# A twelve-part post-norm decoder on one core: cross attention with two bursts and two shared banks, residual normalisations after all four batch elements, the recurrence's buffers inside the sum buffer

## The reference, cut to what matters

```python
sim = einsum(q, k) * 64 ** -0.5        # 512 queries, 154 keys (155 with the null key)
out = einsum(softmax(sim + mask), v)   # then out @ Wo
```

## Time and profile before

| | us |
|---|---|
| median of 3 runs | 6972.68 (6953.23 to 6976.98) |
| the profiled execution | 6962.96 |
| its span in the profile | 6961.2 |
| PE busy in it | 5716.5 |
| mean granted TensorE clock | 0.867 of full |

### The profile page before, as it was taken

The page is one execution under the profiler, slowest core; times in us unless marked ns, Lnnn a source line. Parts: engine busy times, 40 slices in busy tenths (PEclk is TensorE's granted clock), DMA queues, the critical chain, the costliest instruction groups (busy, mean ns, idle before and its releaser), DMA issues. The chain is left out here.

```text
span 6961.2 us, 111729 instructions
## 1 busy us (share of the span) xinstructions
PE 5716.5 (82%) x40346; PEld 3557.6 (51%) x40346; DVE 3487.7 (50%) x7093; ACT 3180.1 (46%) x9357; POOL 2210.9 (32%) x2229
## 2 busy tenths in 40 slices
PE   3898888998988788787887878877778984788888
PEld 2554455555656465464654646547776552223443
DVE  5341354454555364563645636427884445454433
ACT  3342344444456475574755747534441432244422
POOL 0220000001367274672746727406662220000000
PEclk6899898988999899998999989976666996799987
DMA  1000000000011111111111111100000000000000
GB/s 43 1 1 8 13 1 1 1 1 14 1 35 36 31 40 36 35 36 30 41 36 30 41 30 37 40 16 1 1 1 4 1 6 0 7 1 21 1 0 6
DMA packets 28398, 119.49 MB, mean 17 GB/s; under 512 B 5412, under 2 KB 5928, under 8 KB 26024
## 3 DMA queue, kind: packets, MB, share of 16 engines
q1 hardware_dynamic: 27816, 111.97, 5.8%
HBM read 38.55 MB, written 1.05 MB: 6 GB/s over the span
## 5 line engine op out<-in xcount | busy, mean ns | idle before, releaser
L159 POOL MEMSET norm_eps<- 128x1 f32 x44 | 4.3, 98 | 2237.0 <-POOLq L115 2237.0
L1989 POOL TENSOR_TENSOR local_rot<-local_raw,local_cos 128x512 f32<-128x512 f32 x384 | 487.6, 1270 | 301.2 <-DVE local_raw L2033 301.2
L1992 POOL TENSOR_TENSOR local_other<-local_raw,local_sin 128x256 f32<-128x256 f32 x768 | 557.3, 726 | 60.2
L1931 ACT ACTIVATE ps<-ps,local_negmax 128x96 f32<-128x96 f32 x1536 | 488.3, 322 | 37.3 <-DVE local_negmax L2012 36.4
L1854 PE MATMUL ps<-arena,local_xs 128*128 128x512 f32 x768 | 447.0, 666 | 70.2 <-ACT local_xs L1911 51.4
L1995 POOL TENSOR_TENSOR local_rot<-local_rot,local_other 128x512 f32<-128x512 f32 x384 | 487.2, 1269 | 30.1
L1926 ACT ACTIVATE local_squares<-ps 128x512 f32<-128x512 f32 x384 | 230.7, 601 | 508.9 <-PE ps L1854 508.5
L2019 DVE TENSOR_REDUCE local_norm<-local_squares 128x8 f32<-128x512 f32 x384 | 263.4, 686 | 280.4 <-ACT local_squares L1926 280.4
L544 ACT ACTIVATE attn_probs<-attn_shifted,attn_negmax 128x512 f32<-128x512 f32 x256 | 184.9, 722 | 392.5 <-DVE attn_negmax L587 392.5
L587 DVE CUSTOM_DVE_ANT_0 attn_shifted<-arena,ps 128x512 f32<-128x512 f32 x256 | 176.2, 688 | 331.4 <-PE ps L501 331.4
L1842 PE MATMUL ps<-local_K,local_Q 64*64 64x96 f32 x6144 | 337.0, 249 | 0.0
(11 more groups left out here) (490 smaller groups left out, 13280.3 us busy)
## 6 DMA issues: line engine op xcount, KB each, us to landing
local_V_span<-local_V SPq DMA_DIRECT2D x96, 384.0 KB, 4.0
local_V_span<-local_V SPq DMA_DIRECT2D x96, 256.0 KB, 3.6
arena<-in_L1f_a SPq DMA_DIRECT2D x7, 2176.0 KB, 8.7
local_V_span<-local_V SPq DMA_DIRECT2D x72, 128.0 KB, 2.3
arena<-in_L3f SPq DMA_DIRECT2D x1, 3460.0 KB, 11.1
arena<-in_L1f_f SPq DMA_DIRECT2D x6, 537.5 KB, 4.0
arena<-in_L0f SPq DMA_DIRECT2D x1, 2824.5 KB, 9.8
arena<-in_L0x SPq DMA_DIRECT2D x1, 2049.5 KB, 9.0
```

What stands on the lines that cost most here:

```text
L1931: nc.scalar.activation(scores, scores, ACT.Exp, bias=m.negmax[:, s % 2, u:u + 1], accum_out=m.total[:, s % 2, u:u + 1])\
L1989: link(nc.gpsimd.tensor_tensor(rot, raw, m.cos[:, t, a * DH:(a + 1) * DH].unsqueeze(1) .broadcast_to([P, 8, DH]), ALU.mult))
L1992: link(nc.gpsimd.tensor_tensor(other[:, :, lo:lo + HALF], raw[:, :, HALF - lo:DH - lo], m.sin[:, t, a * DH + lo:a * DH + lo + HALF].unsque ...
```

## The change

The sum of a sublayer is kept for every batch element (`core.sums`, and `core.Y` is the current element's part of it). The 20 calls of `residual_norm` are gone; `residual_norm_all(core, core.sums)` stands once behind `rwkv` and once at the end of each of the four sublayers that `each` runs. In `cross_stage` the bank `TAIL` joins `SHARED`: feed pieces, tail transposes and output projections take two banks by turns, and each waits for the use before the last. The values are issued as one burst of four L936 matmuls and one of four L944 matmuls; the latter now take 64 rows each, with `VT` held twice, multiplied by a 0/1 column (`parity`) that keeps the rows of j = 0 or j = 1. The semaphore waits between the segments are gone. With the mask per batch element (L0x) the mask matmul has one row instead of 128, at partition 0 for i = 0 and 64 for i = 1. ACT takes the exponentials ahead of q. In the state-space mixer `first` and the output `Y` are views of `core.sums`.

```diff
-        self.Y = self.buf("Y", [P, S])
+        self.sums = self.buf("sums", [P, B, S])
...
+        self.Y = self.sums[:, b, :]
...
-def residual_norm(core):
-
-    normalize(core, core.X, core.X, add=core.Y[:, :])
...
-    residual_norm(core)
...
         if feeding(s) is not None:
             uses.append(feeding(s))
+        if 0 <= s - TURN < N:
+            uses.append(("tail", s - TURN, 0))
         if projecting(s) is not None:
             uses.append(("out", projecting(s), 0))
...
-        V, VT = tmp("V", [P, 2, INNER]), tmp("VT", [P, 2, QUAD * DH])
+        V, VT = tmp("V", [P, 2, INNER]), tmp("VT", [P, 2, 2, QUAD * DH])
...
-        freed = dict(read, out=y_done)
+        freed = dict(read, out=y_done, tail=tails_ready)
+        first_half = st.sem("first_half")
...
-        SC, PT, TAIL, OUT, SHARED = core.pairs[0:2], core.ps[4], core.ps[5], core.ps[6], core.ps[7]
+        SC, PT, OUT, SHARED = core.pairs[0:2], core.ps[4], core.ps[5], core.ps[6:8]
+
+        def bank(use):
+            return SHARED[use_at[use] % 2]
...
             def wait_for_bank(use):
-                k = use_at[use] - 1
+                k = use_at[use] - 2
                 if k >= 0:
                     pe.wait_ge(freed[uses[k][0]], count(*uses[k]))
...
-                            row = bias[:, qt if mask == "per_query" else b, :]
+                            part = slice(0, P) if mask == "per_query" else slice(DH * i, DH * i + 1)
+                            row = bias[part, qt if mask == "per_query" else b, :]
                             nc.tensor.matmul(SC[n % 2][:, i, 0:2 * keys].rearrange("p (h k) -> p h k", k=keys),
-                                             unit_bf[:, :], row.unsqueeze(1).broadcast_to([P, 2, keys]), start=True,
-                                             stop=False)
+                                             unit_bf[part, :], row.unsqueeze(1).broadcast_to([row.shape[0], 2, keys]),
+                                             start=True, stop=False)
...
                     if n >= 1:
                         pe.wait_ge(pts_ready, n)
-                        pe.wait_ge(tails_ready, n)
                     for g in range(QUAD):
                         nc.tensor.transpose(PT[:, g * P:(g + 1) * P], probs[:, n % 2, g, :], core.ident)
-                    nc.tensor.transpose(TAIL[:, 0:P], ends[:, n % 2, :, :].rearrange("p g k -> p (g k)"),
+                    wait_for_bank(("tail", n, 0))
+                    nc.tensor.transpose(bank(("tail", n, 0))[:, 0:P], ends[:, n % 2, :, :].rearrange("p g k -> p (g k)"),
                                         core.ident).then_inc(turned, 1)
...
-                    for j in range(2):
-                        cols = slice((2 * (quad % 2) + j) * TILE, (2 * (quad % 2) + j + 1) * TILE)
-                        for i in range(2):
-                            h = QUAD * quad + 2 * j + i
-                            nc.tensor.matmul(OUT[DH * i:DH * i + DH, cols], V[:, b % 2, h * DH:(h + 1) * DH],
-                                             pts[:, n % 2, 2 * i + j, :], start=True, stop=False)
-                        if j == 1:
-                            pe.wait_ge(first_pair, n + 1)
-                        elif n >= 1:
-                            pe.wait_ge(values_done, n)
-                        for i in range(2):
-                            part = slice(32 * (2 * i + j), 32 * (2 * i + j) + tail)
-                            mm = nc.tensor.matmul(OUT[DH * i:DH * i + DH, cols],
-                                                  VT[part, b % 2, quad * DH:(quad + 1) * DH], tails[part, n % 2, :],
-                                                  start=False, stop=True)
-                        mm.then_inc(values_done if j == 1 else first_pair, 1)
+                    def place(i, j):
+                        lo = 2 * (quad % 2) + j
+                        return OUT[DH * i:DH * i + DH, lo * TILE:(lo + 1) * TILE]
+                    pairs = [(i, j) for j in range(2) for i in range(2)]
+                    for i, j in pairs:
+                        h = QUAD * quad + 2 * j + i
+                        nc.tensor.matmul(place(i, j), V[:, b % 2, h * DH:(h + 1) * DH], pts[:, n % 2, 2 * i + j, :],
+                                         start=(j == 0), stop=False)
+                    for i, j in pairs:
+                        part = slice(DH * i, DH * i + DH)
+                        mm = nc.tensor.matmul(place(i, j), VT[part, b % 2, j, quad * DH:(quad + 1) * DH],
+                                              tails[part, n % 2, :], start=False, stop=(j == 1))
+                    mm.then_inc(values_done, 1)
...
         @st.block.scalar
         def _(act):
             for s in STEPS:
-                f = feeding(s)
-                if f is not None and f[0] == "q":
...
                             nc.scalar.activation(powers[:, n % 2, g, :], SC[n % 2][:, i, h * keys:(h + 1) * keys],
                                                  ACT.Exp, bias=negmax[:, n % 2, g:g + 1]).then_inc(exp_ready, 1)
+                f = feeding(s)
+                if f is not None and f[0] == "q":
...
+                    nc.scalar.mul(Q[:, b % 2, i, :], bank(f)[:, :], DH ** -0.5).then_inc(read[kind], 1)
...
-                        mm = nc.vector.tensor_copy(VT[:, b % 2, :], out[:, 0:QUAD * DH])
+                        for j in range(2):
+                            own = core.c("parity")[:, j:j + 1]
...
+                                mm = nc.vector.tensor_scalar(VT[:, b % 2, j, :], out[:, 0:QUAD * DH], own, None, ALU.mult)
...
-        Y = tmp("Y", [P, B, S])
+        Y = core.sums
...
-    first, u = buf("first", [P, 2, 4, B, DN]), buf("u", [P, 2, B, 2, SSM_CHUNK])
+    first = core.sums[:, 0:2, :].rearrange("p k (s b n) -> p k s b n", s=4, b=B)
...
         for b in range(B):
             core.work_on(b)
             f(core, b, arena)
+        residual_norm_all(core, core.sums)
...
             rwkv(core)
+        residual_norm_all(core, core.sums)
```

More of the change, by code:

```diff
@@ L823, in cross_stage @@
         if has_null:
-            null_rows = tmp("null_rows", [P, QUAD * DH])
+            null_rows = tmp("null_rows", [P, 2, QUAD * DH])
             loads += QUAD
@@ L839, in _ @@
                     row = 32 * g + tail - 1
-                    sp.dma_start(null_rows[row:row + 1, :], core.dram["null_v"]).then_inc(loaded, 16)
+                    sp.dma_start(null_rows[row:row + 1, g % 2, :], core.dram["null_v"]).then_inc(loaded, 16)
         @st.block.gpsimd
@@ L845, in _ @@
             if has_null:
-                nc.gpsimd.memset(null_rows[:, :], 0.0).then_inc(zeroed, 1)
+                nc.gpsimd.memset(null_rows[:, :, :], 0.0).then_inc(zeroed, 1)
             pool.wait_ge(zeroed, 1)
@@ L890, in _ @@
                     kind, b, i = f
-                    out = SHARED
+                    out = bank(f)
                     ctx = core.context[:, b, :]
@@ L952, in _ @@
                     for c in range(CHUNKS):
-                        mm = nc.tensor.matmul(SHARED[:, 0:TILE], w("Wo", c * P, (c + 1) * P), oT[:, r % 2, c, :],
+                        mm = nc.tensor.matmul(bank(("out", r, 0))[:, 0:TILE], w("Wo", c * P, (c + 1) * P), oT[:, r % 2, c, :],
                                               start=(c == 0), stop=(c == CHUNKS - 1))
@@ L959, in _ @@
             for s in STEPS:
-                f = feeding(s)
-                if f is not None and f[0] == "q":
-                    kind, b, i = f
-                    act.wait_ge(ready[kind], count(kind, b, i))
-                    if b >= 2:
-                        act.wait_ge(scores_ready, U * (b - 1))
-                    nc.scalar.mul(Q[:, b % 2, i, :], SHARED[:, :], DH ** -0.5).then_inc(read[kind], 1)
                 n = s
@@ L976, in _ @@
                                                  ACT.Exp, bias=negmax[:, n % 2, g:g + 1]).then_inc(exp_ready, 1)
+                f = feeding(s)
+                if f is not None and f[0] == "q":
+                    kind, b, i = f
+                    act.wait_ge(ready[kind], count(kind, b, i))
+                    if b >= 2:
+                        act.wait_ge(scores_ready, U * (b - 1))
+                    nc.scalar.mul(Q[:, b % 2, i, :], bank(f)[:, :], DH ** -0.5).then_inc(read[kind], 1)
                 n = s - TURN
@@ L982, in _ @@
                     nc.scalar.copy(pts[:, n % 2, :, :].rearrange("p g q -> p (g q)"), PT[:, :]).then_inc(pts_ready, 1)
-                    nc.scalar.copy(tails[:, n % 2, :], TAIL[:, 0:P]).then_inc(tails_ready, 1)
+                    nc.scalar.copy(tails[:, n % 2, :], bank(("tail", n, 0))[:, 0:P]).then_inc(tails_ready, 1)
         @st.block.vector
@@ L993, in _ @@
                 dve.wait_ge(loaded, 16 * loads)
-                link(nc.vector.tensor_copy(unit_bf[:, :], core.ident))
+                if mask == "per_query":
+                    link(nc.vector.tensor_copy(unit_bf[:, :], core.ident))
+                else:
```

(22 more changed lines are left out.)

1 line of the change is left out of this document (removed).

## The result

The changed kernel takes 6737.74 us (median of 4 runs, 6726.11 to 6747.94) where the kernel before takes 6973.22 beside it: a ratio of 0.9667, 95% interval 0.9643 to 0.9692, or 235 us less. The forecast was 6787, in a range of 6740 to 6855.

A forecast was written before the change was run, and what follows sets the result against it. PE sets the pace in L0x's steady part; start-ups run at half clock, single normalisations are latency-bound. Terms -34.7 - 6.5 + 3.8 - 57 - 33 - 58 = -185 give 6778 from the profiled 6963.0, forecast 6787 us, range 6740 to 6855.

The forecast's parts named there:

- five pipelined stages for 20: Normalisations: 20 single stages of 128.7 us in all become five pipelined ones summing to 94.0, a gain of 34.7 us.
- L0f's restart: L0f: without a normalisation between them, all elements begin at full clock, 6.5 us gained (nothing to 6.5).
- L3f's restart: L3f: elements may gain as L0f's do without normalisations between them; nothing counted.
- L1a without its normalisations: L1a: ACT must load its square-root table while DVE waits, 3 x 1.3 = 3.8 us lost.
- bursts and mask: Cross attentions: four value bursts become two, 0.28 us per unit, and L0x's one-row mask saves 0.12; 57 us (0 to 66).
- banks and start-ups: Cross attentions: two shared banks remove waits for DVE's copy, 33 us; start-ups without gaps reach full clock, 58 us.
- on the clock: Rival: the clock stays at half in the start-ups, gain 26 instead of 58, 6819 us; chance 0.15.
- on the bank: Rival: the second bank only moves the wait to the tail transpose or q's late read, 6820 us; chance 0.07.
- on the bursts: Rival: the bursts give nothing, 0.15 paid elsewhere or saved time becomes evict and POOL waits, 6844 us; chance 0.10.
- the tail burst's halves run one after the other: Rival: a tail burst takes 1.03 us instead of 0.59, 31 us lost over 192 units, 6875 us; chance 0.03.
- The slower rival: Steady parts: PE waits for DVE and POOL and the clock falls to 1.2 GHz, 7152 us; chance 0.02.
- a sign against the forecast: Cross attentions: the forecast is wrong if, among other signs, L936 and L918 wait more than they do now.

The follow-up runs named there:

- e2: Changed kernel with the value matmuls back in the old order of four segments (two whole rows, two tails, twice): 6804.24 us, ratio 0.9764.
- e4: Changed kernel with L0x's mask again as matmuls over 128 rows, unit matrix as other operand: L0x 294.1 us instead of 287.9, one run.
- e3: Changed kernel with one bank for feed pieces and projections and the other for tail transposes, as before the change: 6836.76 us, ratio 0.9820.
- e1: Changed kernel with the whole cross-attention function as before, so only the normalisations change: 6903.78 us, ratio 0.9917.
- e7: Changed kernel with DVE's eviction ahead of the maxima in cross attentions and L1a's square-root table loaded early: 6716.66 us, ratio 0.9636.
- e10: Kernel of e5 (all value matmuls 128 rows by 64 columns) with the four-segment order of e2: 6728.34 us in one run.
- e8: Changed kernel with one kind of burst per stage all on one part of the array, results wrong, for times only: 6824.6 us in one run.
- e9: Changed kernel with e5's and e7's edits, DVE's total ahead of a feed piece's copy, and split waits for POOL's products: 6708.78 us, ratio 0.9618.
- e6: Changed kernel with each burst reordered, both matmuls of one column half and then both of the other: 6750.59 us in one run.
- e5: Changed kernel with tail value matmuls over 128 rows, using four masked copies of the tail values: 6728.6 us, ratio 0.9654.

## Why the forecast was right, and where it was too small

Term by term, in us, from the profiles; the span fell by 224.4 us:

| term | forecast | measured | from |
|---|---|---|---|
| five pipelined stages for 20 | -34.7 | -40.8 | 128.65 to 87.9, the five windows above |
| L0f's restart | -6.5 | -6.5 | four elements of 43.65 |
| L3f's restart | nothing | -3.0 | its elements, 301.4 to 298.5 |
| L1a without its normalisations | +3.8 | -1.0 | its elements, 811.8 to 810.8 |
| bursts and mask | -57 | -63 | e2 and e4, 56.8 + 6.2 |
| banks and start-ups | -33 - 58 | -102 | e3 |
| clock in the cross attentions' old code, at their ends above all | nothing | some -13 | e1 |

Together -229; the untouched L1f and L2a are 7 us longer (3418.3 to 3425.7 from L1f's first attention on), which leaves 2 us untold. ACT's new order, the exponentials ahead of q, was never taken out by itself; the terms of the cross attentions (63, 102 and 13) leave nothing for it in their 175.6.

- **Normalisations.** The step that was mis-sized is "L1a, L2f and L3f ... I take the middle, 18.8". L2f's and L3f's stages take 16.4, L1a's 18.4; RWKV's 20.3, not 21.2. "L3f may gain the same way; I count nothing" gave 3.0.
- **The table load** costs what was said: DVE's wait grows by 4.3 us (5.5 to 9.8), and e7, which hides the load, shortens the three stages by 3.8, the forecast's figure. What was left out is that L1a's elements gain as L0f's do when no normalisation stands before them; that outweighs the load. With the load in them the elements are still 1.0 us shorter in all, so they gain 4.8.
- **Bursts.** Size right (0.29 for a unit by e2, 0.28 forecast; the mask 0.10, 0.12 forecast), and nearly every unit counted: 56.8 of 192 x 0.30, where the forecast had left out some in L1x. The step "a burst costs its streaming and once 0.15 to 0.20, however long it is" had the right number with the wrong cause: e10 has four short segments at the price of one. It is paid at a change of shape.
- **Banks.** The 33 us hold: e3 brings back 7.7 and 3.3 us of waits in L0x. Outside the start-ups e3 costs 102.3 - 61.8 = 40.5 us: 34.5 in the steps with these waits, where the clock stays full, and 5.9 in the first four steps of the stages, which in e3 begin at half clock (2.7 in L0x, 0.8 in L1x, 2.3 in L2x). The forecast had 2 for L1x and nothing for the other two.
- **Start-up.** 60 us, 58 forecast, by the mechanism forecast: without the gaps the clock is full for good 3.6 us into the stage in L1x, 5.4 in L2x and 13.5 in L0x, whose pause for a DMA comes first.
- **What was not in the sum at all**: the low clock at the end of each cross attention. The last parts take 62.5 us together in the kernel before, 46.2 in the changed one; in e1, with the old code, they take 53.1, so more than half of the gain comes without any change to the cross attention. That it fell this way was luck: nothing in the forecast said so, and why the clock holds in one stretch and falls in its equal is not shown.

On the rivals: those on the clock, on the bank and on the bursts are refuted by e3 and e2. That the tail burst's halves run one after the other is refuted by its 0.59 us, against e8, which shows what one after the other would take, 1.01. The Trainium skill (TensorEngine Tiling, Gotcha 1: PSUM Pressure) says that different row tiles cannot access one PSUM bank at the same time. These tail matmuls are on two row tiles (and on different columns), write one bank (to different partitions), and the measurement disagrees: 0.59 us. The slower rival did not come: the granted clock of the steady part is 1.00. One thing went as I had named it as a sign against the forecast: L916 waits more for POOL than L918 did, by 3.6, 3.3 and 2.1 us in the three steady parts. The waits for the eviction fell by 6.4 together, so the two kinds add up to 2.6 us more, little beside the 175.6.

The forecast's range was too narrow at the low end. It took the clock's behaviour "elsewhere" as 10 us; the ends of the cross attentions alone gave 9 by e1, and between the changed kernel and e9 one untouched stretch, L3a and L3x, moved by 17.

## What to carry to other kernels

Count the changes of shape in the order of PE's matmuls, not the bursts: a change between whole rows and tails cost about 0.15 us here. Matmuls on different parts of the array ran together in either order tried, and padding a small operand with zeros to the neighbour's shape was cheaper than switching. Where PE waited for a bank's reader behind every piece, in the start-ups, the gaps cost twice, once as idle time and once as clock, and a second bank was worth about double its waits. In the steady part, at full clock with or without them, it was worth the waits alone. When a change shortens a kernel with many stages, compare the stages one by one: the clock of the untouched ones moved here by as much as a small change gains.

## What the runs showed of the hardware that was not expected

- Four value matmuls on two column halves take 0.59 us in alternating order and 0.59 in turn (e6), and 1.02 on one half (e8): the order of issue plays no part in a burst of this length.
- Padding pays: tails over 128 rows instead of 64 shorten a unit from 1.18 to 1.03 us (e5), and four alternating segments of one shape take the same 1.03 (e10) where two shapes take 1.46 (e2).
- The clock can fall inside a steady part: in L2x of the kernel before it is 0.50 for 6.8 us although PE was never idle for more than 1.2 us at a time just before.
- The same code differs by the clock that it finds: L3a and L3x, the same 3209 matmuls, take 647.7 to 664.9 us over the kernels here, with a mean granted clock of 0.93 and 0.90, and the end of L0x in its old code 16.3 or 21.7. Why the clock falls in one and not in the other of two equal stretches, these runs do not tell.
